# Four weight buffers in the feed-forward stage, bias matmuls that wait tile by tile, and the last pass moved into the last column block

## The reference

```
x = x + layernorm(attn(layernorm(x)))          # attn: long convolution along the last axis, + D * u
x = x + layernorm(ffn(layernorm(x)))
# attn: a kernel K of length 4096 is made from Lambda, p, q, B, Ct (64 states) by an inverse FFT;
#       y = irfft(rfft(u, 8192) * rfft(K, 8192))[..., :4096] + D * u
# ffn:  x @ kernel + bias                                  (4096 x 4096)
#       + B_eff @ (A_eff @ x)  + B_shared @ (A_shared @ x) (LoRA, rank 32, one adapter per batch row)
```

## Time and profile before

| | us |
|---|---|
| median of 3 runs | 2123.95 (2120.29 to 2128.22) |
| the profiled execution | 2118.09 |
| its span on the slowest core (core 7) | 2116.6 |
| spans of the eight cores | 2096.9 to 2116.6 |
| TensorE busy with matmuls | 991.2 (47%) |
| VectorE, ScalarE busy | 424.5, 318.5 |
| GpSimd busy (issuing DMAs) | 167.3 |

### The profile page before, as it was taken

The page is one execution under the profiler, slowest core; times in us unless marked ns, Lnnn a source line. Parts: engine busy times, 40 slices in busy tenths (PEclk is TensorE's granted clock), DMA queues, the critical chain, the costliest instruction groups (busy, mean ns, idle before and its releaser), DMA issues.

```text
span 2116.6 us, 13038 instructions; the slowest of 8 cores (2096.9 to 2116.6 us)
## 1 busy us (share of the span) xinstructions
PE 991.2 (47%) x4229; PEld 411.9 (19%) x4229; DVE 424.5 (20%) x762; ACT 318.5 (15%) x386; POOL 167.3 (8%) x313
## 2 busy tenths in 40 slices
PE   4451000626647357265466767666666666630000
PEld 0000000312323223133222222222222222210000
DVE  0222541243232422333301010101010101011221
ACT  1400000232232332323201010101010101010111
POOL 0002111000000000000011111111111111100000
PEclk9999999958668577586799999998989998975555
DMA  0000645021120220201024343333333333346555
GB/s 6 1 0 11 116 64 97 29 79 30 50 80 1 80 80 1 80 15 66 40 40 80 40 80 45 78 45 75 47 75 47 77 46 74 48 137 238 218 204 212
DMA packets 66580, 149.79 MB, mean 71 GB/s; under 512 B 16727, under 2 KB 50056, under 8 KB 60576
## 3 DMA queue, kind: packets, MB, share of 16 engines
q0 software_dynamic: 41248, 45.82, 15.3%
q1 hardware_dynamic: 25266, 103.14, 13.6%
HBM read 137.08 MB, written 52.23 MB: 89 GB/s over the span
## 4 chain that ended last, share of the span: by engine, by line
PE 37%; DMA 31%; DVE 14%; ACT 8%; issue 7%; DVEq 1%; SPq 1%; POOL 1%; ACTq 0%; POOLq 0%
DMA wbuf<-wk 17%; PE pffn L834 15%; PE pconv L726 13%; DMA xb<-f_scr 5%; DMA y<-ya 2%; DVE trv L761 2%; DVE trv L682 2%; DVE xb L754 2%; DVE ya L886 2%; PE ptrb L778 2%; DMA f_scr<-fstage 1%; PE putil L360 1%; ACT n1b L690 1%; ACT ya L751 1%; ACT n1b L769 1%
## 5 line engine op out<-in xcount | busy, mean ns | idle before, releaser
L834 PE MATMUL pffn<-wbuf,n2fm 128*128 128x512 bf16 x2048 | 506.2, 397 | 222.0 <-DMA wbuf<-wk 221.0
L834 PEld LDWEIGHTS pffn<-wbuf,n2fm 128*128 128x128 bf16 x2048 | 192.7, 101 | 538.3 <-issue 369.0
L726 PE MATMUL pconv<-tband,xfmt 128*128 128x512 bf16 x1152 | 265.6, 395 | 8.1 <-DVE xfmt L711 8.1
L829 POOL DMA_DIRECT2D wbuf<-wk x256 | 135.1, 528 | 1370.7 <-PE pffn L834 1354.3
L849 DVE TENSOR_SCALAR_CACHE_REDUCE fstage<-pffn 128x512 f32<-128x512 f32 x64 | 44.3, 692 | 778.8 <-PE pffn L840 763.3
L853 ACT ACTIVATE tra<-fstage 128x512 bf16<-128x512 f32 x64 | 40.3, 629 | 792.2 <-DVE fstage L849 786.8
L726 PEld LDWEIGHTS pconv<-tband,xfmt 128*128 128x128 bf16 x1152 | 115.8, 101 | 156.0 <-issue 31.0
L778 PE MATMUL ptrb<-idsb,n1b 128*128 128x128 bf16 x256 | 32.9, 310 | 195.6 <-ACT n1b L769 195.6
L707 PE MATMUL ptrb<-idsb,n1b 128*128 128x128 bf16 x256 | 29.8, 308 | 184.8 <-ACT n1b L690 183.2
L730 DVE SCALAR_TENSOR_TENSOR ya<-n1b,dbc,pconv 128x512 f32<-128x512 bf16 x64 | 47.9, 748 | 225.8 <-PE pconv L726 225.8
L735 ACT ACTIVATE tra<-ya 128x512 bf16<-128x512 f32 x64 | 40.3, 629 | 275.3 <-DVE ya L730 275.3
(11 more groups left out here) (208 smaller groups left out, 564.1 us busy)
## 6 DMA issues: line engine op xcount, KB each, us to landing
wbuf<-wk POOLq DMA_DIRECT2D x256, 128.0 KB, 2.9
xb<-u SPq DMA_DIRECT2D x8, 2048.0 KB, 14.5
x_scr<-xb SPq DMA_DIRECT2D x8, 2048.0 KB, 9.1
f_scr<-fstage SPq DMA_DIRECT2D x64, 256.0 KB, 2.8
xb<-x_scr SPq DMA_DIRECT2D x8, 2048.0 KB, 8.0
xb<-f_scr SPq DMA_DIRECT2D x8, 2048.0 KB, 13.1
y<-ya SPq DMA_DIRECT2D x8, 2048.0 KB, 6.3
n1b<-lora_b POOLq DMA_DIRECT2D x16, 256.0 KB, 3.7
```

The costliest lines, as they stand in the source:

```text
L726: tg = E("tensor", lambda t, g=g, ij=ij, j0=j0: t.matmul(out=pconv[g % 3][:, :], lhsT=xfmt[:, 128 * ij:128 * ij + 128], rhs=tband[:, j0:j0 ...
L829: t_wload[kg] = DMA("gpsimd", f"wload{kg % 2}", lambda g, f=f, oc=oc, kg=kg: g.dma_start(out=wbuf[kg % 2][:, :], in_=wk[128 * f:128 * f + ...
L834: tlast = E("tensor", lambda t, f=f, t2=t2, kg=kg: t.matmul(out=pffn[t2][:, :], lhsT=bass.AP(n2fm, TOK * f + P * t2, [[FC * TOK, P], [1, P]]),
```

## The change

It has three parts, all in the feed-forward stage and the tail.

1. `wbuf` has four buffers instead of two, and the request for step `kg` waits for step `kg - 4`.
2. The bias matmul of token tile `t2` waits for the eviction of `pffn[t2]` alone.
3. The tail's body for a token tile stands inside the last column block (`oc == 7`), right behind that tile's store. Its loads wait for the eight stores of that tile's rows and for the output store of the tile before. The stores to `f_scr` count on a semaphore for each token tile (`frow{t2}`) instead of one for each staging buffer (`fout{i}`), and the wait for a staging buffer is put on the former.

```diff
-        wbuf = [e(nc.sbuf_tensor(f"wbuf{i}", [P, 512], BF16)) for i in range(2)]
+        wbuf = [e(nc.sbuf_tensor(f"wbuf{i}", [P, 512], BF16)) for i in range(4)]
...
         for oc in range(8):
-            toks = [t_bhl, t_axb, tc["ones2b"]] + ps1_clear
-            if oc > 0:
-                toks += [t_fev[(oc - 1, t2)] for t2 in range(TT)]
-            W("tensor", toks)
+            W("tensor", [t_bhl, t_axb, tc["ones2b"]] + ps1_clear)
             for t2 in range(TT):
+                if oc > 0:
+                    W("tensor", [t_fev[(oc - 1, t2)]])
                 E("tensor", lambda t, t2=t2, oc=oc: t.matmul(
...
-                war = [t_ffmm[kg - 2]] if kg >= 2 else []
+                war = [t_ffmm[kg - 4]] if kg >= 4 else []
                 W("gpsimd", war)
-                t_wload[kg] = DMA("gpsimd", f"wload{kg % 2}", lambda g, f=f, oc=oc, kg=kg: g.dma_start(
+                t_wload[kg] = DMA("gpsimd", f"wload{kg % 4}", lambda g, f=f, oc=oc, kg=kg: g.dma_start(
...
                 if idx >= 4:
-                    war = [t_fst[idx - 4], t_fsq[idx - 4]]
+                    rprev = (idx - 4) % TT
+                    rec = pr.dsems[f"frow{rprev}"]
+                    war = [(rec[0], rec[1]), t_fsq[idx - 4]]
                 W("vector", [t_dl] + war)
...
-                t_fst[idx] = DMA("sync", f"fout{sbuf_i}", lambda s, t2=t2, oc=oc, sbuf_i=sbuf_i: s.dma_start(
+                t_fst[idx] = DMA("sync", f"frow{t2}", lambda s, t2=t2, oc=oc, sbuf_i=sbuf_i: s.dma_start(
                     out=f_scr[P * t2:P * t2 + P, 512 * oc:512 * oc + 512], in_=fstage[sbuf_i][:, :]))
-
-        t_p2v = pr.now("vector")
-        t_p2a = pr.now("scalar")
-        t_fout_all = [(pr.dsems[k][0], pr.dsems[k][1]) for k in pr.dsems if k.startswith("fout")]
-        t_yst = [None] * TT
-        for t_i in range(TT):
-            war = [t_p2v, t_p2a, t_x1store[TT - 1]] + t_fout_all
-            if t_i >= 1:
-                war.append(t_yst[t_i - 1])
-            W("sync", war)
+                if oc == 7:
+                    t_i = t2
+                    war = [t_p1v, t_p1a, t_x1store[TT - 1]]
+                    war += [t_fst[o2 * TT + t_i] for o2 in range(8)]
+                    if t_i >= 1:
+                        war.append(t_yst[t_i - 1])
+                    W("sync", war)
...
```

More of the change, by code:

```diff
@@ L814, in build_nc @@
         t_ffmm = {}
+        t_p1v = pr.now("vector")
+        t_p1a = pr.now("scalar")
+        t_yst = [None] * TT
         kglob = 0
         for oc in range(8):
-            toks = [t_bhl, t_axb, tc["ones2b"]] + ps1_clear
-            if oc > 0:
-                toks += [t_fev[(oc - 1, t2)] for t2 in range(TT)]
-            W("tensor", toks)
+            W("tensor", [t_bhl, t_axb, tc["ones2b"]] + ps1_clear)
             for t2 in range(TT):
+                if oc > 0:
+                    W("tensor", [t_fev[(oc - 1, t2)]])
                 E("tensor", lambda t, t2=t2, oc=oc: t.matmul(
@@ L826, in build_nc @@
                 kg = kglob
-                war = [t_ffmm[kg - 2]] if kg >= 2 else []
+                war = [t_ffmm[kg - 4]] if kg >= 4 else []
                 W("gpsimd", war)
-                t_wload[kg] = DMA("gpsimd", f"wload{kg % 2}", lambda g, f=f, oc=oc, kg=kg: g.dma_start(
-                    out=wbuf[kg % 2][:, :], in_=wk[128 * f:128 * f + 128, 512 * oc:512 * oc + 512]))
+                t_wload[kg] = DMA("gpsimd", f"wload{kg % 4}", lambda g, f=f, oc=oc, kg=kg: g.dma_start(
+                    out=wbuf[kg % 4][:, :], in_=wk[128 * f:128 * f + 128, 512 * oc:512 * oc + 512]))
                 W("tensor", [t_wload[kg]])
@@ L835, in build_nc @@
                         out=pffn[t2][:, :], lhsT=bass.AP(n2fm, TOK * f + P * t2, [[FC * TOK, P], [1, P]]),
-                        rhs=wbuf[kg % 2][:, :], start=False, stop=False))
+                        rhs=wbuf[kg % 4][:, :], start=False, stop=False))
                 t_ffmm[kg] = tlast
@@ new lines, in build_nc @@
+                if oc == 7:
[5 more added lines that the diff above has]
+                    W("sync", war)
+                    t_x1l = DMA("sync", "x1in", lambda s, t_i=t_i: s.dma_start(
+                        out=xb[0][:, :], in_=x1_scr[P * t_i:P * t_i + P, :]))
+                    t_fl = DMA("sync", "fin", lambda s, t_i=t_i: s.dma_start(
+                        out=xb[1][:, :], in_=f_scr[P * t_i:P * t_i + P, :]))
+                    W("vector", [t_fev[(7, t_i)]])
+                    t_fs = E("vector", lambda v, t_i=t_i: v.tensor_scalar(
+                        out=trv[:, 0:8], in0=fsums[t_i][:, :], scalar1=1.0, scalar2=None, op0=OP.mult, op1=OP.add,
+                        accum_out=stf["s1"][:, :]))
+                    W("vector", [t_fsq[7 * TT + t_i]])
+                    t_fq = E("vector", lambda v, t_i=t_i: v.tensor_scalar(
+                        out=trv[:, 8:16], in0=fsqs[t_i][:, :], scalar1=1.0, scalar2=None, op0=OP.mult, op1=OP.add,
+                        accum_out=stf["q1"][:, :]))
+                    t_rf, t_nbf = ln_finalize(stf, D, t_fs, t_fq)
+                    W("scalar", [t_nbf, t_fl])
+                    t_lnf = E("scalar", lambda s: s.activation(
+                        out=xb[1][:, :], in_=xb[1][:, :], func=AF.Identity, bias=stf["nbias"][:, :], scale=stf["rstd"][:, :]))
+                    W("vector", [t_lnf, t_x1l] + ([t_yst[t_i - 1]] if t_i >= 1 else []))
+                    t_add = E("vector", lambda v: v.tensor_tensor(out=ya[:, :], in0=xb[0][:, :], in1=xb[1][:, :], op=OP.add))
+                    W("sync", [t_add])
+                    t_yst[t_i] = DMA("sync", "yout", lambda s, t_i=t_i: s.dma_start(
+                        out=y_out[P * t_i:P * t_i + P, :], in_=ya[:, :]))
```

## The result

The changed kernel takes 1854.46 us, the median of 8 runs (1847.98 to 1857.03), against 2123.72 before in the same comparison: a ratio of 0.8723, 95% interval 0.8707 to 0.874. The forecast was 1831 with a range of 1806 to 1905. The profiled execution took 1848.84 us; its slowest core is core 1, not core 7 as before. Now and then an execution is some per cent slower with a lower mean clock on one die; ratios leave those out and medians do not, so a ratio is not always the quotient of two medians.

What follows compares the result with a forecast made beforehand. The prediction took TensorE's waits for weight loads through two buffers as the feed-forward stage's bound. 2118.1 - 292.0 (stage) - 0.6 (tail) = 1825.5, with the median 5.9 above the profiled run: 1831 us, range 1806 to 1905.

Steps and rivals of the forecast that it cites:

- The likeliest case: With four weight buffers TensorE bounds the feed-forward blocks: 1831 us, own range 1812 to 1850, chance 0.68.
- The start of the stage: The first block's feed-forward matmuls start at 1063.45 us, as in the profile before the change.
- The step of 1.72 us: Feed-forward loop: eight matmuls of a step take TensorE 1.72 us instead of 2.85, so 32 steps take 55.0.
- The loads: Weight loads in the feed-forward loop overlap and keep up with TensorE; landing 2.9 us, up to 4.1 allowed.
- the ring: Weight buffer reuse, matmuls to request to next matmuls: 5.70 us, over four steps 1.43 each, leaving 1.2 us of slack.
- The boundary: Between column blocks: first `L840` to first `L834` takes 9.0 us instead of 12.1, bias matmuls running beside evictions.
- The clock after the boundary: After each block boundary TensorE's clock still falls to the 1.2 GHz level, costing 2.2 us a block.
- The tail: Last pass moved inside the last block: -5.5 and +4.9 us, together -0.6.
- The early start: Tail: tile 0's loads wait only for their own eight stores and go out 5.5 us earlier.
- The small store behind `y`: Tail: the new store before the next loads costs 0.7 us a tile, +4.9 over seven, bounds 0 and +19.6.
- slower loads: Rival, chance 0.12: weight loads slower than TensorE in the feed-forward loop; at 2.0 us a step +72, 1903 us.
- A lower grant in the dense stretches: Rival, chance 0.10: clock grant under 1.00 in the feed-forward loop; at 0.83 throughout +90, 1921 us.

Runs made afterwards that it cites:

- e5: Changed kernel with three extra 128x512 matmuls behind each wait of the bias matmuls of token tiles 0 to 6: 1842.80 us, ratio 0.8631.
- e7: Changed kernel with eight weight buffers and the first and last four steps of a block done token tile by token tile: 1807.61 us, ratio 0.8465.
- e1: Kernel before with four weight buffers instead of two and nothing else: 1864.51 us, ratio 0.8769.
- e4: Changed kernel without its third part, the last pass standing behind the loop over the blocks as before: 1851.48 us, ratio 0.8692.
- e3: Changed kernel with three weight buffers instead of four: 1890.02 us, ratio 0.8874.
- e6: Changed kernel whose tail loads no longer wait for the output store; only the f load waits for its eight stores: 1849.72 us, ratio 0.8659.

## Why the prediction was right, and where 23 us went

The likeliest case came true: TensorE is the bound of the blocks. The time of 1854.46 us lies inside the stated range, but 4 us outside the 1812 to 1850 that the prediction gave this case alone. The span was forecast at 1824 and is 1847. Step by step, on core 1:

*The start of the stage*, +9. The prediction took 1063.45 from core 7. Core 1 is later, and later than it was before. The first rows are of core 1 before the change, the second of core 1 after:

```profile
1063.24 3.57 PE L822 MATMUL pffn<-bhl,ones2bs 2*128 2x512 bf16 x8 [1.64 <-DVE axb L796]
...
1066.74 5.88 PE L834 MATMUL pffn<-wbuf,n2fm 128*128 128x512 bf16 x16
```

```profile
1069.17 3.57 PE L824 MATMUL pffn<-bhl,ones2bs 2*128 2x512 bf16 x8 [1.64 <-DVE axb L796]
...
1072.67 9.55 PE L836 MATMUL pffn<-wbuf,n2fm 128*128 128x512 bf16 x33
```

5.9 us of it arose in parts that the change does not touch. Over the eight cores the mean shift is 2.6 us. That a forecast takes its start from one core and is measured on another was not in the range of any term. On core 7, whose rows it used, the span is 1837.4, 13.4 over the forecast: +6.8 for the start, +8.2 for the blocks, -1.6 for the tail.

*The step of 1.72 us*: right to half a per cent. The windows have 48 matmuls in 10 us; the 32 steps without a fall of the clock take 55.4 us (e5), forecast 55.0. Over eight blocks that is +3.

*The loads*: right in the median, 3.1 us to landing where the ring allows 4.1:

```profile
wbuf<-wk POOLq DMA_DIRECT2D x256, 128.0 KB, 3.1
```

There were exceptions that the prediction had not. Two steps still waited, and GpSimd's rows in front of them say why:

```profile
1301.21 1.59 POOL L831 DMA_DIRECT2D wbuf<-wk  x3 [3.87 <-PE pffn L836]
...
1304.30 1.89 PE L836 MATMUL pffn<-wbuf,n2fm 128*128 128x512 bf16 x8 [1.14 <-DMA wbuf<-wk]
...
1526.84 1.58 POOL L831 DMA_DIRECT2D wbuf<-wk  x3 [3.87 <-PE pffn L836]
...
1531.02 1.25 PE L836 MATMUL pffn<-wbuf,n2fm 128*128 128x512 bf16 x3 [2.21 <-DMA wbuf<-wk]
```

The waits are 1.1 and 2.2 us on core 1, and 3.7 us with what lies under the records. It is not the loads that were slow: GpSimd paused 3.87 us where it pauses 1.20 in the rows above, and then sent three requests in a row, so the first came 2.7 us late. The same two bursts, from the same request on (the 114th and the 224th), stand in the trace of all eight cores, and in the traces of all the other runs with four buffers. The ring has GpSimd answer at once, and its slack of 1.2 us does not cover such a pause. Eight buffers do: in e7 one of 3.77 us is in the trace and no matmul waits. Why GpSimd pauses there is open.

*The boundary*: 9.0 forecast, 8.8 in the row above, 8.8 to 9.4 over the seven of core 1, 9.1 on average. e1 against e4 gives its worth by itself: 22.4 us of waits.

*The clock after the boundary*: it fell, as forecast. Its cost is 2.8 us in the row above, 18.0 in the eight blocks of core 1 or 2.25 each, 2.2 forecast; e5 took it away. A block with its boundary is (1601.07 - 1195.91) / 6 = 67.5 us, forecast 66.2. The 7.8 us that all blocks are over are these: about 3 from the steps, 3.7 from the two late requests, 0.5 from the boundaries and 0.4 from the clock.

*The tail*: forecast -0.6, from +4.9 and -5.5. The early start is 6.1 (5.5 forecast). The small store behind `y` was mis-sized for this core. On core 1 the seven times from `y` to the next loads are 8.6 to 9.0 us, 61.3 together. Before, core 7 had 46.7 together: not 6.4 each, as the prediction read from one tile, but 6.4 at five, 7.5 and 7.2 at two. That is +14.6 where +4.9 was forecast, inside the bounds of 0 and 19.6. The rest of a tile's pass got 3.8 us shorter in all, for which the prediction had nothing, so the tail is 245.6 against 240.5: +5.1.

The trace has two reasons for the 8.6 to 9.0. The small store lands about 1 us after `y` (7.6 to 8.1 us after its own issue, 0.8 behind `y`), and `y` itself lands in 7.3 to 7.7 us, while the last `y`, with no small store behind it, takes 6.3. Core 0 has only the first: its `y` lands in 6.3 us, the small store 6.1 us after its issue, and the loads go out after 7.1, just the 0.7 of the forecast. Six of the eight cores have 7.1 to 7.5, core 7 has 8.4 to 8.8 at four tiles of seven. A slow `y` does not need the small store: before, cores 3 and 6 already have 7.2 and more, and in e4 cores 3 and 7 have mostly 6.9 to 7.5 at tiles where the others have 6.3 to 6.6. Why single cores pay more than others was not tested. The mean tail of the eight cores is 236.2 us, against 238.3 before and 238.2 in e4, so on average the moved tail does about what the prediction had, and the slowest core gets nothing of it.

The sum of the three: +9.2 for the start, +7.8 for the blocks (528.4 instead of 520.7), +5.7 for the tail: 22.7 us.

The rivals: slower loads did not occur (e3 shows where they would begin). A lower grant in the dense stretches is in no trace either: the windows of the f loop stand at 1.00 on a program with eight busy cores, and all cores of all profiled executions here show only the two levels 0.50 and 1.00. The 0.83 of the earlier trace rows, which the prediction took as a lower grant, is thus a window with a third of it at the low level. The rule of the Trainium skill (TensorE: Matmul & The Clock Gate, Part 1) about 13/16 of the clock once three cores of a die run dense matmuls would have given 1933 us by the prediction's estimate. The traces do not show it, neither in the stretches of 55 us of the changed kernel nor in e7, whose trace has all eight cores at 1.00 for 495 us on end.

## What to carry to other kernels

Close the ring before touching anything else: the time from the release of a buffer to the first use of its next content, divided by the number of buffers, against the time of one step; here 5.70 / 2 is the kernel before, from which the ring was read, 5.70 / 3 gave 1900 us (1890 measured), and 5.70 / 4, which is under 1.72, gave 1860 for the buffers alone (1865 measured). A ring needs slack for single late requests too: four buffers still lost 3.7 us to two of them. Once the loads are hidden, the ends of a block are next, and they cost twice, as a wait and as a low clock after it; doing the last and the first steps tile by tile removed both here, with the same matmuls. In the chain of load, compute and store of this tail, halves of a tile that wait only for themselves brought 71 us, where the two reorderings of whole tiles (the moved tail and e6) brought nothing clear of the noise. A small store that a load must wait for is better not queued behind a large one.

Read idle time with care: where records of an engine overlap, as TensorE's do, short waits count as busy. In e3 nearly half of the waits were hidden so; the count of matmuls in a window at a grant of 1.00 gave them away.

## What the runs showed that was not expected

Bias matmuls whose weights have only two rows, one each 0.82 us, did not keep the clock up; three full 128x512 matmuls in each of the same gaps did (e5). Whether it is the two rows or the idle time between them is open.

A store of 256 KB issued 0.8 us after a store of 2048 KB and followed by a load of 2048 KB landed 10.1 to 10.7 us later (e6, core 3), without the load beside it 7.6 to 8.1 (the changed kernel, core 1), and 2.8 in the median before. Here a small transfer took the time of what was around it.

GpSimd pauses 3.87 us before the same two of its 256 requests, on all cores and in all traces of kernels with four buffers, and then sends three in a row. The trace shows no cause for the pause.
